# Two Mamba layers on one core: VectorE makes the next step's u*B before it takes the second half of a finished sum

## The reference, cut to what matters

```
def step(h, inp):
    d_t, B_t, x_t, C_t = inp
    dA = jnp.exp(d_t[..., None] * A)
    h = dA * h + (d_t * x_t)[..., None] * B_t[:, None, :]
    y = jnp.einsum('bdn,bn->bd', h, C_t)
    return (h, y)
y = ys + x * D
y = y * silu(z)
return y @ W_out
```

## Time and profile before

| | us |
|---|---|
| median of 3 runs | 2034.77 (2033.21 to 2038.48) |
| profiled execution, its own time | 2036.81 |
| its span, first to last instruction | 2034.9 |
| GpSimd busy | 1937.6 (95%) |
| TensorE busy | 1833.8 (90%) |
| VectorE busy | 1787.9 (88%) |
| ScalarE busy | 1149.4 (56%) |
| mean granted TensorE clock | 0.974 |

### The profile page before, as it was taken

The page is one execution under the profiler, slowest core; times in us unless marked ns, Lnnn a source line. Parts: engine busy times, 40 slices in busy tenths (PEclk is TensorE's granted clock), DMA queues, the critical chain, the costliest instruction groups (busy, mean ns, idle before and its releaser), DMA issues. The chain is left out here.

```text
span 2034.9 us, 16945 instructions
## 1 busy us (share of the span) xinstructions
PE 1833.8 (90%) x4972; PEld 686.9 (34%) x4972; DVE 1787.9 (88%) x1063; ACT 1149.4 (56%) x1179; POOL 1937.6 (95%) x853
## 2 busy tenths in 40 slices
PE   7899889898899899899899889989989988987778
PEld 3333333333343233233333333323323323332332
DVE  3889897868989988987898997998798999699998
ACT  4657565657657446654756745744584574554332
POOL 1999999999999999999999999999999999999997
PEclk9899999999999899999999999999999999999899
DMA  5558558665766877676776787776666677667676
GB/s 148 206 203 210 208 206 208 207 225 180 191 240 217 202 231 255 174 233 212 210 199 219 214 222 233 228 201 243 212 172 207 224 208 215 233 219 207 210 224 153
DMA packets 127623, 427.86 MB, mean 210 GB/s; under 512 B 18524, under 2 KB 23020, under 8 KB 127532
## 3 DMA queue, kind: packets, MB, share of 16 engines
q1 hardware_dynamic: 127532, 426.79, 68.9%
HBM read 416.29 MB, written 6.29 MB: 208 GB/s over the span
## 5 line engine op out<-in xcount | busy, mean ns | idle before, releaser
L987 POOL TENSOR_TENSOR ring<-ring,c_ring 128x1024 f32<-128x1024 f32 x575 | 1346.2, 2369 | 38.3 <-DVE ring L932 33.0
L560 PE MATMUL y_ps<-ring,wp 128*128 128x512 f32 x2304 | 1148.3, 616 | 10.9 <-DVE yv_rows L912 4.5
L932 DVE TENSOR_TENSOR_SCAN ring<-a_ring,b_ps 128x1024 f32<-128x1024 f32 x368 | 841.1, 2286 | 31.6 <-issue 0.5
L560 PEld LDWEIGHTS y_ps<-ring,wp 128*128 128x128 f32 x2304 | 428.1, 194 | 522.5 <-issue 439.8
L932 DVE TENSOR_TENSOR_SCAN ring<-b_ps,b_ring 128x1024 f32<-128x1024 f32 x208 | 471.1, 2274 | 75.1 <-ACT b_ps L732 26.5
L980 POOL TENSOR_TENSOR b_ring<-u_ab,b_ring 128x1024 f32<-128x1024 f32 x161 | 381.9, 2372 | 8.9 <-DMA b_ring<-bc_rows 8.9
L541 PE MATMUL b_ps<-b_in,sel 96*64 96x512 bf16 (+1 forms) x1020 | 230.3, 402 | 143.5 <-DVE ring L932 141.8
L732 ACT ACTIVATE a_ring<-delta_ab,wp 128x1024 f32<-128x1024 f32 x223 | 251.9, 1140 | 158.4 <-DVE ring L932 155.2
L897 DVE TENSOR_TENSOR b_ps<-u_ab,b_ps 128x1024 f32<-128x1024 f32 x223 | 270.3, 1212 | 64.6 <-PE b_ps L541 56.5
L732 ACT ACTIVATE b_ps<-delta_ab,wp 128x1024 f32<-128x1024 f32 x161 | 179.8, 1117 | 208.3 <-DVE ring L932 207.8
L725 ACT ACT_TABLE_LOAD x186 | 238.6, 1283 | 52.7 <-DVE ring L932 49.8
(11 more groups left out here) (97 smaller groups left out, 849.5 us busy)
## 6 DMA issues: line engine op xcount, KB each, us to landing
c_ring<-bc_rows SPq DMA_DIRECT2D x384, 512.0 KB, 4.7
c_ring<-bc_rows SPq DMA_DIRECT2D x384, 256.0 KB, 4.4
b_ring<-bc_rows SPq DMA_DIRECT2D x161, 512.0 KB, 5.3
b_ring<-bc_rows SPq DMA_DIRECT2D x94, 256.0 KB, 5.4
out<-io SPq DMA_DIRECT2D x16, 192.0 KB, 5.0
bc_rows<-bc_out SPq DMA_DIRECT2D x22, 128.0 KB, 5.3
io<-x SPq DMA_DIRECT2D x6, 384.0 KB, 6.2
b_in<-parts SPq DMA_DIRECT2D x24, 96.0 KB, 2.3
```

Of the source, the lines that this page charges most:

```text
L560: nc.tensor.matmul(half(y_ps[:, :], j), ident, half(ring[:, g % RING, :], j), start=(n == 0 and kind == FWD), stop=(n == NS - 1)).then_inc ...
L932: nc.vector.tensor_tensor_scan(out=h, data0=a, data1=b, initial=0.0, op0=ALU.mult, op1=ALU.add).then_inc(h_ready, 1)
L987: nc.gpsimd.tensor_tensor(r, r, c, ALU.mult).then_inc(g_ready, 1)
```

## The change

At each step VectorE's `ahead` phase comes before `take_1` in place of after it. Only the list of VectorE changes; every instruction, operand and semaphore stays.

```
-DVE_ORDER = ("take_0", "scan", "take_1", "ahead", "jobs", "last")
+DVE_ORDER = ("take_0", "scan", "ahead", "take_1", "jobs", "last")
```

## The result

The median after is 2048.82 us (four runs, 2046.96 to 2052.97), beside 2034.73 (2033.21 to 2038.48) for the kernel before: a ratio of 1.0066 [1.0054, 1.0079]. That is 14.1 us lost where 3.2 were forecast, and beyond the upper end of the range, 2045.0. The profiled execution took 2046.96, the lowest of its four, with a span of 2045.1 us; so the two traces, with spans 10.2 apart, show some 10 of the 14 us.

What follows compares the result with a forecast made beforehand. GpSimd (95% busy) and VectorE (88%) were taken as near the bound, TensorE's late B mattering where VectorE waits. Terms 0.84 + 0.78 + 0.89 + 0.5 + 0.7 - 0.54 = 3.2 on 2034.77 gave 2038.0 us; range 2031.0 to 2045.0.

Steps and rivals of the forecast that it cites:

- VectorE's 0.18: VectorE's three instructions at a turn take 3.91 us in place of 4.09, a gain of 0.18 at 26 of 29 turns.
- TensorE's delay: The take starts 1.12 us later, and TensorE's second half at 19 turns passes all of it on.
- The sum: Turn-by-turn losses less gains, counted where GpSimd soon waits for a scan: a net loss of 3.2 us.
- Turns whose g+2 is GpSimd's: B stays early enough and VectorE keeps 0.18; gains reach GpSimd at 958.8, 1453.0 and 1782.0: -0.54 us.
- at most 1.12 - 0.43 = 0.69: Turn at 462.9: delay passed through TensorE's chain, less a 0.43 pause, to a wait at 479.62; taken at 0.5 us.
- The terms for 1833.7 and 1886.5: Turns with half clock today: about 0.4 us of a later start is left at 1833.7, 0.3 at 1886.5.
- Turns whose g+2 is VectorE's: VectorE waits for a late B: 0.28 us lost at 792.2, 1287.5, 1935.6; 0.39 at third tiles 843.8 and 1986.0.
- The turn at 219.6: TensorE has only a 0.23 pause up to a B that VectorE awaits, so 0.89 us is lost.
- about 5.8: Sign to look for: VectorE's wait of 4.94 us for B behind the turn at 219.6 becomes about 5.8.
- The turns not named: At all remaining turns GpSimd's backlog covers 0.2 to 0.4 us, so they lose 0.
- The rival: TensorE falls to half clock between its halves as idle time grows; 2049.4 us, or 2043.7 half covered; chance 0.24.
- A mean clock clearly under 0.974: Sign that, with half clock behind turns, would show the slower half-clock rival.

Runs made afterwards that it cites:

- e1: Kernel before, VectorE's order kept; at the 29 turns TensorE's second half also waits for u*B of the next step: 2052.29 us, 1.0094.
- e12: Repeat of e6, the new order at only the 15 turns whose step g+2 is GpSimd's, on the chip of e9: 2042.03 us, 1.003.
- e6: Kernel before with the new order at only the 15 turns whose step g+2 is GpSimd's: 2042.83 us, 1.0031.
- e9: As e6, plus one to three zero matmuls filling TensorE's idle time before the second half at ten of those turns: 2035.12 us, 1.0003.
- e2: Kernel after, with two or three zero matmuls between TensorE's halves where it has no jobs (9 of the 29 turns): 2046.82 us, 1.0071.
- e5: Kernel before with the new order at only the 14 turns whose step g+2 is VectorE's: 2042.22 us, 1.0035.
- e10: Kernel after, with TensorE spreading B of step g+2 before the second half as in e3, and the zero matmuls of e9: 2035.39 us, 0.9995.
- e3: Kernel after, with TensorE spreading B of g+2 before the second half, acting at the 14 turns where g+2 is VectorE's: 2038.29 us, 1.0022.
- e7: Kernel before with the edit of e3, B of step g+2 spread ahead of the second half, as a control: 2033.68 us, 0.9993.
- e8: Kernel before with the edit of e2, zero matmuls between TensorE's halves, as a control: 2037.94 us, 1.0014.
- e4: Kernel before with both takes put in front of the scan on VectorE: 2039.68 us, 1.0023.
- e11: The kernel of e4, both takes ahead of the scan, run again for a second profile: 2039.18 us.

## Why the prediction was wrong

**VectorE's 0.18.** Right in the trace: 3.91 us a turn in place of 4.09 at 26 of the 29 turns. At the other three u*B waited for its B (4.13 at 895.5 and 1389.7, 6.32 in place of 5.95 at 331.1). The rows decided rightly: the operation behind u*B starts after 1.12 us where it needs nothing of it, after 1.31 where it waits for it. The Trainium skill, "VectorE: DVE Perf Modes", section "The DRAIN you can't avoid", does not speak against the gain as the prediction has it, for it also says that a next operation that is not held starts earlier. That agrees with a take that starts 1.12 us behind the start of a 1.21 us u*B. Its sentence that the semaphore costs nothing extra does not agree with the 1.31.

**TensorE's delay.** Right in size (idle 0.82 became 1.95), and by itself enough for the loss, as e1 shows.

**The step that failed: half clock was put at nothing.** The sum priced the delay as if TensorE stayed at full clock behind it, but for 0.7 us at two turns, and left the half clock to a rival. It failed at both kinds of turns.

*Turns whose g+2 is GpSimd's.* "Its B stays early enough; VectorE keeps the 0.18" was to gain 0.54. These 15 turns cost 6.2 to 7.4 us (e12, e6), and with the idle time filled and the second half as late the loss is gone (e9). At full clock the step was right at 1782.0, where VectorE in e9 waits for nothing. The term "at most 1.12 - 0.43 = 0.69", taken at 0.5, for 462.9 was worth 3.50 in the kernel after, with two falls; in e9, without them, 0.14. The terms for 1833.7 and 1886.5, 0.7 together, measured -0.41 and -0.07 in the kernel after, as the clock had fallen there before the change too, and 1.12 and 1.61 in e12.

*Turns whose g+2 is VectorE's.* At full clock these terms were about right: 0.33 and 0.31 at 792.2 and 1287.5 and 0.32 at 1935.6 (e2) for 0.28 each, 0.42 (e5) and 0.45 at 843.8 and 1986.0 for 0.39. But the 14 turns cost 6.7 (e5) where the terms sum to about 2.5 (0.84 + 0.78 + 0.89). Some of the rest is the fall at 1935.6, 1.88 in place of 0.32. How the whole of it splits between the delay and half clock no run isolates; with B spread first and the zeros, both are undone (e10).

*Terms that were too small at full clock.*

- The turn at 219.6: 0.89 forecast, 1.45 measured, and 1.16 in e2, which has no fall there. The wait that was to become "about 5.8" stayed at 4.94; it moved 1.12 later as a whole. GpSimd's wait behind it went from 1.65 to 3.07.
- "The turns not named have a backlog that covers 0.2 to 0.4 us: 0". At 730.6, 1123.0, 1226.0, 1560.5 and 1615.5 the difference grows by 0.13 to 0.7, alike in the kernel after, e9 and e12, 1.8 to 1.9 us together.

The 1.61 behind 1389.7 can't be put down to the delay. It goes with the half clock some 33 us behind the turn at 1337.9: where that lasts 6.8 us (after, e1, e2, e5, e9), 1.48 to 1.61; where 3.4 (before, e3, e7, e8, e12), -0.18 to 0.07; where there is none (e4, e6, e10, e11), -1.21 to -1.59. In e9 that turn is as before, so the late B isn't needed for it. Likewise the 1.48 behind 1337.9, forecast at 0, is found with half clock of 6.8 us from 18 us ahead of that turn (after, 1.43 in e2, and 0.92 in e8, where the zeros delay the half by 0.73); with the late B but without that half clock it is 0.25 (e5) and 0.41 (e1). What sets the length is open.

**The rival.** Half clock was named, with its place and a price near the truth (2049.4, against 2048.8), and given 0.24. That agreement is partly luck: the price counted 12 falls at 0.95 on top of the 3.2, while there were fewer falls, of very different price. Two things spoke against it too loudly. The first was a single stretch without a fall, at 219.20 behind 2.96 us of idle time: in the kernel after the same place, behind the same 2.96, opens the first half in 1.91 us in place of 1.10. The fall there is not the change's, as e6 and e12, with the order of before at that turn, have it too. One turn without a fall in one execution shows only that a fall need not come. The second was the sign to look for, "A mean clock clearly under 0.974": after has 0.971, but e1 has 0.975 with the greatest loss of all and falls at the turns at 462.9, 1453.0 and 1782.0 too, and e9 and e12 have the same 0.973, one with the loss and one without. Where the half clock lies counts, not how much of it there is. The rule cited from "TensorE: Matmul & The Clock Gate", section "HAM oscillation — how this bites in real kernels", in the Trainium skill, that bursts with waits between them bring the half clock back, is told there of longer waits, for a DMA. Here it agrees with e12 at 1782.0 (2.80 us idle, then 0.50) and with e9 (0.23 idle, then 1.00), but "each time" does not hold: in the kernel after no fall follows the 1.95 us of idle time at 843.8, 1337.9 and 1986.0.

## What to carry to other kernels

When an instruction that frees a buffer moves later, look at what is queued behind the engine that waits for the buffer, and at the idle time that it gets there: the first passes the delay on, the second can halve the clock of the work behind. A stretch without a fall of the clock in one trace is weak evidence against a fall in the changed kernel; price it at every turn where the idle time grows. And before a difference of one or two microseconds between two traces is put down to a change, look where the half clock lies in either of them.

## What was not expected of the hardware

Where matmuls with weights of zero fill TensorE's idle time at the turn at 1782.0, the granted clock stays at 1.00 (e9); with the idle time in their place it is 0.50 behind it (e12). Three such matmuls, six in the profile, take 2.74 us. They do not always help: in e10 the clock falls at the turn at 1833.7 just ahead of the same three, which then take 4.13 us and make the second half 1.3 later. And a fall comes or not from one execution to the next: at the turn at 958.8 the trace of e6 has one within 7 us of the scan's start, and the trace of e12, from the same program, has none.
